# Weight loads of the later layers move to GpSimd's queue, and the orders are planned anew

## What is computed

```python
mod = (cond_global @ adaLN_W + adaLN_b)[:, None, :]
sh_msa, sc_msa, g_msa, sh_x, sc_x, g_x, sh_mlp, sc_mlp, g_mlp = jnp.split(mod, 9, axis=-1)
x_norm = _ln(x, norm1_w) * (1 + sc_msa) + sh_msa
...
self_out = _attn(q, k, v, attn_mask[None, None]).reshape(b, s, d) @ attn_out_W
x = x + g_msa * self_out
xc = _ln(x, normc_w) * (1 + sc_x) + sh_x
qc = (xc @ cq_W).reshape(b, s, H, HD)
kc = (cond_tokens @ ck_W).reshape(b, LC, H, HD)
vc = (cond_tokens @ cv_W).reshape(b, LC, H, HD)
cross = _attn(qc, kc, vc, cond_kv_mask[:, None, None, :]).reshape(b, s, d) @ co_W
x = x + g_x * cross
xm = _ln(x, norm2_w) * (1 + sc_mlp) + sh_mlp
h = jax.nn.gelu(xm @ mlp_W1 + mlp_b1, approximate=True)
return x + g_mlp * (h @ mlp_W2 + mlp_b2)
```

## Time and profile before

| | |
|---|---|
| median of 3 runs | 2713.38 us (2712.58 to 2728.46) |
| the profiled execution | 2724.64 us |
| its span, first to last instruction | 2722.9 us |
| mean granted TensorE clock | 0.961 |
| TensorE / VectorE / ScalarE / GpSimd busy | 95% / 65% / 55% / 24% |
| instructions | 55574 |
| moved by DMA | 342.69 MB, mean 126 GB/s |

### The profile page before, as it was taken

The page is one execution under the profiler, slowest core; times in us unless marked ns, Lnnn a source line. Parts: engine busy times, 40 slices in busy tenths (PEclk is TensorE's granted clock), DMA queues, the critical chain, the costliest instruction groups (busy, mean ns, idle before and its releaser), DMA issues.

```text
span 2722.9 us, 55574 instructions
## 1 busy us (share of the span) xinstructions
PE 2592.7 (95%) x19774; PEld 1871.0 (69%) x19774; DVE 1772.4 (65%) x4435; ACT 1510.7 (55%) x2471; POOL 658.4 (24%) x650
## 2 busy tenths in 40 slices
PE   7789999999999999989999999999999999999987
PEld 5557777777776766656677777776776777777766
DVE  4467656755765565777675767675776777677741
ACT  1335566566565554445666666655655555655562
POOL 2013212212222222212222222222332232323220
PEclk9889999999999987888999999999999999999988
DMA  6344334334334454545343434343334343434310
GB/s 201 117 132 131 117 103 146 101 103 139 108 102 131 150 183 138 175 159 166 109 153 102 146 114 148 113 142 112 116 118 153 101 144 98 135 108 147 94 62 16
DMA packets 317577, 342.69 MB, mean 126 GB/s; under 512 B 90874, under 2 KB 208474, under 8 KB 316988
## 3 DMA queue, kind: packets, MB, share of 16 engines
q1 hardware_dynamic: 284860, 292.06, 34.5%
q10 hardware_dynamic: 32256, 47.07, 4.8%
q0 software_dynamic: 192, 0.01, 0.0%
HBM read 203.42 MB, written 118.31 MB: 118 GB/s over the span
## 4 chain that ended last, share of the span: by engine, by line
PE 76%; DVE 12%; SPq 3%; issue 3%; DMA 3%; ACT 2%; POOL 0%; ACTq 0%; DVEq 0%; POOLq 0%
PE gen L1342 12%; PE gen L1351 11%; PE gen L1238 11%; PE gen L1204 11%; PE gen L1322 10%; DVE row_max L1671 5%; PE score L1296 4%; PE score L1251 3%; PE score L1280 3%; PE score L1266 3%; PE score L1302 3%; PE gen L1213 3%; DVE xhat L1586 1%; DVE max_tok L1686 1%; DVE stats L1574 1%
## 5 line engine op out<-in xcount | busy, mean ns | idle before, releaser
L1489 ACT ACTIVATE probs<-score 128x1024 f32<-128x1024 f32 (+1 forms) x576 | 572.3, 1027 | 331.0 <-PE score L1296 216.1
L1671 DVE TENSOR_REDUCE row_max<-score 128x4 f32<-128x1024 f32 (+1 forms) x640 | 648.5, 1044 | 139.8 <-PE score L1280 95.6
L1342 PE MATMUL gen<-xnT,w_w1M 128*128 128x256 f32 x1536 | 374.3, 393 | 2.2 <-ACT xnT L1429 2.2
L1351 PE MATMUL gen<-w_w2M,hT 128*128 128x256 f32 x1536 | 354.7, 385 | 3.0 <-ACT hT L1513 3.0
L1342 PEld LDWEIGHTS gen<-xnT,w_w1M 128*128 128x128 f32 x1536 | 284.9, 193 | 65.1 <-issue 18.2
L1351 PEld LDWEIGHTS gen<-w_w2M,hT 128*128 128x128 f32 x1536 | 286.5, 191 | 56.9 <-issue 18.3
L1523 POOL TENSOR_TENSOR rstd<-var_eps,minus_half 128x2 f32<-128x2 f32 x160 | 112.4, 703 | 864.2 <-DVE var_eps L1580 863.9
L1531 POOL TENSOR_TENSOR xnT<-xnT,xhat 128x512 f32<-128x512 f32 x112 | 142.5, 1272 | 597.0 <-DVE xhat L1700 578.3
L1498 ACT COPY oT<-gen 128x512 f32<-128x512 f32 x224 | 132.0, 589 | 218.6 <-PE gen L1322 210.8
L1429 ACT ACTIVATE xnT<-gen,mod_all 128x256 f32<-128x256 f32 x288 | 147.0, 568 | 181.3 <-PE gen L1213 180.0
L1720 DVE TENSOR_TENSOR xhat<-gen,gate 128x256 f32<-128x256 f32 (+1 forms) x112 | 60.1, 537 | 228.0 <-PE gen L1351 154.8
(11 more groups left out here) (160 smaller groups left out, 4131.0 us busy)
## 6 DMA issues: line engine op xcount, KB each, us to landing
q_stack<-parts_scratch SPq DMA_DIRECT2D x336, 256.0 KB
parts_scratch<-parts ACTq DMA_DIRECT2D x160, 256.0 KB, 2.5
parts_scratch<-parts SPq DMA_DIRECT2D x160, 256.0 KB, 2.6
k_self<-parts_scratch SPq DMA_DIRECT2D x144, 256.0 KB, 3.9
k_cross<-parts_scratch SPq DMA_DIRECT2D x192, 78.0 KB, 2.4
xnT<-oT SPq DMA_DIRECT2D x224, 64.0 KB, 1.8
x_scratch<-x SPq DMA_DIRECT2D x48, 256.0 KB, 3.3
x_in<-x_scratch SPq DMA_DIRECT2D x48, 256.0 KB, 2.8
```

What stands on the lines that cost most here:

```text
L1342: mm = pe.matmul(buf[:, i * S:i * S + S], w["M"]["w1"][:, fc, col:col + P], xnT[s][:, fc, :], start=fc == 0, stop=fc == FC - 1)
L1351: mm = pe.matmul(buf[:, 0:D], hT[:, j, c * P:c * P + P], w["M"]["w2"][:, j, :], start=j == 0, stop=j == FFC - 1)
L1489: act.activation(probs[st.probs][0:keys, :, :], score[st.fill.buf][0:keys, :, :].rearrange("p a (r q) -> p (a r) q", r=2), ACT.Exp, bias=k ...
L1671: dve.tensor_reduce(dst, src, AX_X, ALU.max).then_inc(max_done[b], 1)
```

## The change

It does four things. The steps `ldw` that wait for former users run on GpSimd's queue instead of SyncE's; the function `load_weights` moves there word for word. These loads raise semaphores of their own, `w_renewed`, one for each area, so that the two queues don't count on one. The planner charges any transfer by `ISSUE` on whatever engine it stands (2.5 us for an `ldw`, whatever its DMAs). And `FIRST` has new constants, 30 in place of 26, so that all five orders are planned anew.

```diff
--- before.py
+++ after.py
@@ -103,7 +103,7 @@
 HOP = {"pe": 0.29, "act": 0.21, "dve": 0.14, "pool": 0.12, "sp": 0.1}
 TABLE = 1.28
 TRANSFERS = ("ldx", "ldc", "ldg", "stx", "zq", "sm", "sd", "sg", "sh", "ldw", "ph", "pw", "lh", "ll", "la", "ms")
-FIRST = {"ce": 15.3, "dv": 0.7, "ex": -9.3, "ge": 5.3, "hi": 11.9, "ldc": 8.9, "ldg": 13.3, "ldx": 13.4, "lh": -6.3, "ln": -5.3, "lo": 0.5, "mr": 2.3, "out": 3.8, "ph": -2.2, "pv": -6.8, "pw": 2.6, "qkv": -6.1, "rp": -8.7, "rt": -6.9, "sd": -0.6, "stx": 4.2, "up": -1.9, "ve": -10.0, "xT": -2.5, "xe": 8.2, "zq": 13.4}
+FIRST = {"ce": 15.3, "down": -2.7, "dv": 0.7, "ex": -9.3, "ge": 5.3, "hi": 11.9, "ldc": 11.5, "ldg": 2.4, "ldx": 9.3, "lh": -9.1, "ll": -5.2, "ln": -5.3, "lo": 0.5, "mr": 0.2, "out": 3.8, "ph": -2.2, "pv": -6.8, "pw": 2.6, "qkv": -6.1, "res": 2.1, "rp": -11.0, "rt": -6.9, "sd": 0.4, "sg": 1.2, "stx": 1.7, "up": -1.9, "ve": -11.4, "xT": -2.5, "xe": -4.9, "zq": -8.7}
 MARGIN, AGE, STAY = 1.4, 16, 4
 ISSUE = {"ldw": 2.5, "la": 0.5, "ms": 0.4, "zq": 0.55, "lh": 1.27, "ll": 0.63, "sm": 0.56, "sd": 0.53, "sg": 1.08, "sh": 0.53}
 TILES = {"S": "rows", "ST": "rows", "W": "columns"}
@@ -251,7 +251,7 @@
             before = blk.behind or max(((i, n) for i in range(li + 1) for n in range(len(LAYERS[i]))
                                         if (i, n) < (li, k) and LAYERS[i][n].area == blk.area), default=None)
             users = [self.ends[PLACE[before[0], seq], before[1]] for seq in range(B)] if before else self.late_users.get(blk.area, [])
-            self.weights[li, k] = self.add(PLACE[li, 0], k, blk, "ldw", 0, "sp", users)
+            self.weights[li, k] = self.add(PLACE[li, 0], k, blk, "ldw", 0, "pool" if users else "sp", users)
             if not users:
                 self.load_early(self.weights[li, k])
 
@@ -461,7 +461,7 @@
                 took, wants = st.cost + switch(st),  {"ex": "exp", "ge": st.blk.gelu}.get(st.name)
                 if wants and wants != table:
                     table, took = wants, took + TABLE
-                busy[eng] = now + (took if eng != "sp" and st.name != "ph" else ISSUE.get(st.name, 0.43))
+                busy[eng] = now + (took if st.name not in TRANSFERS else ISSUE.get(st.name, 0.43))
                 events.append((busy[eng], None))
                 events.append((now + took + HOP[eng], st))
             if started:
@@ -612,6 +612,7 @@
                       ("L3", "mlp"): {"b2": "L3_b2", "b1": "L3_b1"}}
 
         w_loaded = {area: sem(f"w_loaded_{area}") for area in AREAS}
+        w_renewed = {area: sem(f"w_renewed_{area}") for area in AREAS}
         x_loaded = [sem(f"x_loaded{i}") for i in range(X_IN)]
 
         def out_rows(tile, src):
@@ -649,15 +650,15 @@
             return bias_tile(blk, {"self": "so", "cross": "co", "mlp": "b2"}[blk.kind])
 
 
-        counted, loads_through = dict.fromkeys(AREAS, 0), {}
-        for blocks in LAYERS:
-            for blk in blocks:
-                counted[blk.area] += 16 * len(weight_dmas(blk))
-                loads_through[blk] = counted[blk.area]
+        counted, loads_through = {}, {}
+        for li, blocks in enumerate(LAYERS):
+            for k, blk in enumerate(blocks):
+                loaded = (w_loaded if plan.weights[li, k].early else w_renewed)[blk.area]
+                counted[loaded] = counted.get(loaded, 0) + 16 * len(weight_dmas(blk))
+                loads_through[blk] = loaded, counted[loaded]
 
         def weights_loaded(blk):
-            return w_loaded[blk.area], loads_through[blk]
-
+            return loads_through[blk]
 
         hT = sb("hT", [P, FFC, S])
         wide = {"w1": w["M"]["w1"][:, :, 0:3 * D], "w2": w["M"]["w2"][:, 0:6, :].rearrange("p (c g) d -> p c (g d)", c=FC),
@@ -1115,18 +1116,6 @@
                     sp.wait_ge(*moved(ends_in(st.job)))
                     dst = a["out"] if st.li == len(LAYERS) - 1 else x_dram
                     sp.dma_start(dst[st.seq].rearrange("(c p) d -> p c d", p=P), x[s][:, :, :]).then_inc(x_stored[s], 16)
-
-                def load_weights(st):
-                    if st.li == 0:
-                        for sums in st.after:
-                            sp.wait_ge(*filled(sums))
-                    else:
-                        done = max(st.after, key=lambda res: res.nth_all)
-                        sp.wait_ge(*moved(done.fill))
-                    if st.blk.of == "L1":
-                        sp.wait_ge(late_gates_stored, 16 * (N_GATE - GATES_EARLY))
-                    for dst, src in weight_dmas(st.blk):
-                        sp.dma_start(dst, src).then_inc(w_loaded[st.blk.area], 16)
 
                 def load_late(st):
 
@@ -1170,8 +1159,6 @@
                         place_sums(st)
                     elif st.name == "sh":
                         place_heads(st)
-                    elif st.name == "ldw":
-                        load_weights(st)
                 for s in range(SLOTS):
                     sp.wait_ge(x_stored[s], 16 * len(range(s, len(LAYERS) * B, SLOTS)))
 
@@ -1515,6 +1502,18 @@
 
             @block.gpsimd
             def _(pool):
+                def load_weights(st):
+                    if st.li == 0:
+                        for sums in st.after:
+                            pool.wait_ge(*filled(sums))
+                    else:
+                        done = max(st.after, key=lambda res: res.nth_all)
+                        pool.wait_ge(*moved(done.fill))
+                    if st.blk.of == "L1":
+                        pool.wait_ge(late_gates_stored, 16 * (N_GATE - GATES_EARLY))
+                    for dst, src in weight_dmas(st.blk):
+                        pool.dma_start(dst, src).then_inc(w_renewed[st.blk.area], 16)
+
                 n_gated, read = 0, None
                 for st in plan.order["pool"]:
                     s, blk = st.slot, st.blk
@@ -1538,6 +1537,8 @@
                         pool.wait_ge(crossed, n)
                         pool.wait_ge(*moved(turn.fill))
                         pool.tensor_tensor(value, value, other, ALU.add).then_inc(rotated, 1)
+                    elif st.name == "ldw":
+                        load_weights(st)
                     elif st.name == "xb":
                         pool.wait_ge(xhat_ready, of(st, "nx").nth_all)
                         if st.k == 0 and st.job >= SLOTS:
```

## The result

The changed kernel takes 2728.26 us (median of 20 runs), the kernel before, run beside it, 2719.09 us (20 runs). The ratio is 1.0031, with a 95% interval of 1.0018 to 1.0044: 8.4 us slower, 5 to 12. One of the changed kernel's runs took 3188 us at a granted clock of 0.74; such slow runs are left out of every ratio here. I had said 2697 us, and 2670 to 2719. Within 1% it is, but the sign is the other one, and the range missed it. The base moved too: I had counted from the median of three runs, 2713.38 us, and twenty give 2719.09, 5.7 us more. That alone would not have saved the forecast: 8.4 us above 2713.38 is 2722, still outside the range.

What follows compares the result with a forecast made beforehand. TensorE, busy 2592.7 of 2722.9 us, was taken as the bound, so only its idle and low-clock time could be won. Terms -5 - 5.7 - 4.8 + 1.6 + 1 - 3 = -15.9 us took 2713.4 to 2697 us, range 2670 to 2719.

Steps and rivals of the forecast that it cites:

- The order: New constants decide TensorE's order over 816 to 1360 us alone; distances that matter hardly change, so 0 was taken.
- Rival 2: New order pays: a quarter of remaining idle and clock loss from 816 to 1360 us, 24 us, giving 2673; chance 0.21.
- rival 3: New order costs the same quarter from 816 to 1360 us, giving 2721; chance 0.08, with mixtures up to 2740.
- The move: Nine weight sets, 44 DMAs, go from SyncE's queue to GpSimd's; gains and costs sum to -15.9 us.
- Gain at 78 us: TensorE's wait for adaln3b: its DMA goes out 4.5 us earlier, and small matmuls behind run faster; -5 us.
- Gain at 866 us: Context DMA goes out earlier, so both TensorE gaps go, -5.7 us, and the low clock behind them, -4.8 us.
- rival 1: The gaps move to the next late input, such as VectorE's residual at 866; half the gains gone, 2705 to 2718; chance 0.25.
- Costs at 851 and 934 us: GpSimd's rstd waits behind six weight DMAs, so TensorE's transpose waits: 1.6 us at 851, 1 us at 934.
- Gain at 2050 us: TensorE's wait for keys: store goes out about 1 us earlier, loads 1 us faster, clock 1 us; -3 us.
- GpSimd's issues: Each weight DMA issue on GpSimd was taken at 0.72 us, from its 722 ns bias loads.
- Rival 4: Slow GpSimd issues hold rstd behind each set; gains eaten at 1.75 us each, 2743 at 3.6 us; chance 0.06.

Runs made afterwards that it cites:

- order_only: The changed kernel's orders on all engines, but the nine later weight sets still issued by SyncE; ratio 1.0049 to the kernel before.
- move_only: The kernel before with all its orders kept, only the nine later weight sets moved to GpSimd's queue; ratio 0.9999 to the kernel before.
- before_down: The kernel before with the one new constant `down` -2.7 (second MLP projection) for jobs 0 to 11; ratio 1.0112 to the kernel before.
- after_early_two: The changed kernel with constants `down` and `xe` back at their old values for jobs 0 to 10; ratio 0.9972 to the kernel before.
- before_late_loads: The kernel before with first-layer MLP and third-layer self-attention weights later in SyncE's queue; ratio 0.9970 to the kernel before.

## Why the prediction was wrong

**The order: this step failed.** I wrote of 204 to 816 us that "There no order can win anything", which is true, and then counted the new order at 0, although TensorE's order differs from 257 us on. A full stretch can't be won, but it can be lost: that TensorE had 2.7 us of idle in 612 was the merit of the old constants. order_only puts the term at +13 us (8.4 to 18.5) in place of 0: about 19 us lost in layer 0 (23.0 against move_only's 3.9 at 849 us), and some 6 won back in layer 1. Rival 2 (order pays) and rival 3 (order costs) may both have come true, in different layers; I had put both in the same one. And comparing median distances between steps was too coarse: the pairs of jobs would have been seen by listing the ends of the jobs in the planned order, which needs no trace. The planner had an answer ready, too. The length that it simulates is 2611.0 us for the order of before, 2615.1 for that of after and 2628.9 for before_down: it sets these three in the order in which the runs do, though the distances are too small. It doesn't see everything: after_early_two, which the runs have 7.6 us ahead of before, it puts 1.4 us behind.

**The move: -15.9 us predicted, -0.3 us measured** (-5.4 to +4.6, move_only). Term by term:
- *Gain at 78 us, -5.* The issue came earlier, as worked out, by 4.2 us in after and 3.0 in move_only. But "Its landing still competes with the 2 MB, as before" was mis-sized: the landing grew from 6.5 to 10.3 and 9.9 us, and the gap went from 7.08 to 6.94 and 6.92 us. The term is 0. The shares of the DMA queues from 75 to 85 us in after say why: the software queue (GpSimd's) took 47.0% of the 16 engines' time, the hardware queue 53.8.

```profile
q1 hardware_dynamic: 1599, 1.89, 53.8%
q0 software_dynamic: 487, 1.67, 47.0%
```

- *Gain at 866 us, -10.5.* The context's wait went, VectorE's did not: 0.75 + 1.80 us of the 5.7 remain. The clock behind them was the larger error: with the cost at 858 taken off, some 3.5 us were won where I had counted 10.5. The granted clock there is 0.79 from 872 to 888 us in move_only, after 0.70 from 868 to 885 in before. It is rival 1 here, and even the half that rival 1 left was too much. (Half of the 18.5 us of gains is 9.3, not the 8 that rival 1 was counted at.)
- *Costs at 851 and 934 us, +1.6 and +1.* Measured 2.02 and 2.22 us in move_only: the mechanism and the first size were right, the second left out the addition of x that stands ahead of rstd.
- *Gain at 2050 us, -3.* Measured -0.05 us in move_only (3.73 us), +1.5 in after, where the store that the scores need landed in 10.8 us instead of 7.8. The Trainium skill, DMA: Bandwidth & Descriptors, section Queues, rings and completion order, has each DMA engine go round its queues; the shares of 47.0 and 53.8% agree with that. But that the whole gap would go by it, as I had written beside it, did not come: with the engines full, the queue of the 2 MB takes 47.0% of their time from the small transfers, just when they are needed.
- *GpSimd's issues, 0.72 us assumed.* 0.54 to 0.94 us. Rival 4 is out: the longest of the 44 issues took 0.94 us, where 1.75 would have been needed. The 3100 ns that the Trainium skill names (SBUF — State Buffer, section SBUF: two separate sides) are seen in none of the 44.

By these rows the move sums up to 0 - 3.5 + 2.0 + 2.2 + 0 = +0.7 us, and the timed -0.3 agrees. So the sum had two faults of about equal weight. The move missed by some 16 us: 8 of them at 78 and 2050, where I counted issue times and what ended last was bandwidth, 7 at 866, where VectorE's next wait and the clock behind it kept most of the gain, and 1 to 2 in the costs. The order, taken as 0, was 13 us. Together that is 5 us more than the 24 by which the forecast missed, the same 5 us that the move may win in the new order. Neither fault alone would have left the range (2713 and 2710 us; by the base of twenty runs the first comes to 2719, its very edge).

## What to carry over

When a plan is searched anew, compare it over the stretches that are full as well: there it can only lose, and one constant lost 12 us. Before moving an issue to another queue, ask whether the transfer waits for its issue or for bandwidth; if the DMA share is near 1 while it travels (here 0.99 in before from 78 to 85 us), delay the big transfer that nobody needs yet (before_late_loads, 0.9970) and mind what it meets at its new place. And whether a gain behind a loss is the loss given back is told by a deliberate delay of known size, timed, not by two profiles.

## What was not expected of the hardware

With full DMA engines the arrival of a transfer hardly depended on the queue of its competitor, or on when it was issued: adaln3b, begun between 74.5 and 78.7 us, was there at 84.7 to 85.5 us in four kernels. And in layer 1, where TensorE waits often, the granted clock of one kernel's execution can hide or feign 5 to 8 us: before and after differ by 0.6 us in their profiles and by 8.4 in twenty runs each.
